# A wavelet-attention convolution block: the map convolution by six products for four outputs, with the next step's column filter in two lumps

## The chip, the cores and the metric

The kernel runs on one core of a Trainium2 chip. The metric is device time in microseconds (us) for one execution. Engines: PE (TensorE, matmuls; PEld is its weight load), DVE (VectorE), ACT (ScalarE), POOL (GpSimd), SP (SyncE, which only issues DMAs here).

## The reference, cut to what matters

```
# x: (8, 64, 224, 224); layer: x + block(group_norm(x)); W = H = 224, C = 64
res = conv3x3(x, W_id, b_id)                       # all 8 images
cA, cH, cV, cD = _swt2_level3(x[0])                # image 0 alone: row and column filters
high = jnp.stack([cH, cV, cD], axis=1).reshape(1, C3, H, W)
low_att = _attention(cA[None], DCT_LOW, ...)       # 1x1 convolution times a scale per channel
high_att = _attention(high, DCT_HIGH, ...)
dmt = jnp.concatenate([low_att, high_att], axis=1) # 256 channels
out = leaky_relu(conv3x3(dmt, W_enc, b_enc), 0.01) # one 64-channel map
return out + res                                   # the map is added to every image
```

The filtered image 0 has four subbands of 64 channels. The 3x3 convolution of these 256 channels to 64 gives the map `e_map` (128 lanes: 64 channels times 4 rows above, 4 rows below in a step), which the last stage adds to every image. "Map convolution" below is this one.

## The kernel before, in words

The program is three blocks one after the other, with a barrier between them.

`before_maps` (L204 to L710) filters image 0 along the rows on PE in four parts (`k`), writes the result to DRAM (`scratch`, the tensor `row_filtered`), and works out the attention scales and the merged convolution weights in small steps put between the filter's matmuls.

`encoder` (L713 to L930) makes the map in NE = 28 steps of ER = 8 rows. All engines walk through the steps in program order and meet by semaphores only. In step `step`:
- SP: `load(u)` (L752) brings the row-filtered rows of chunk `u = step + 2` into one of two buffers `s_in`; then `load_stats(k)` (L759) brings four pieces of the other seven images for their group-norm statistics, into two buffers `sx`. SP issues in this order and stands still at each wait: `load_stats(k)` waits until DVE has used piece `k - 2` (`stat_used`, L761), `load(u)` until POOL has split an earlier chunk (`s_split`, L777).
- POOL: `normalise` (L188; scale L199, bias L201) on chunk `u`, then the low half of its fp16 split (L928), after ACT's high half (`split_hi`, L844).
- PE: `gen` (L785, matmul L798), the column filter, makes one row of two subband pairs, 448 columns, in nine matmuls; eight rows a step, through a ring of four PSUM banks. Then `conv` (L802, matmuls L810 and L815) for q = 0, 1: 27 weight taps by two pairs, each on two column halves of the array, 448 columns each, and the bias.
- ACT `hi` (L839) and DVE `lo` (L874) turn each generated row into an fp16 pair in `d`; ACT carries the last two rows over (L861); ACT L869 and DVE L916 turn a finished accumulation into the leaky ReLU and store it in `e_map`.
- DVE `take_stats` (L879, statistics L885) works through four pieces a step, four instructions each.

`main` (L933 to L1173) runs the 3x3 convolution of all eight images and adds `e_map` to each. It is not touched.

What sets the order around the change is the queue of each engine as written, above all SP's:

```
for step in range(NE):
    u = step + 2
    ...
        load(u)
    for k in range(CPS * step, min(CPS * step + CPS, NCK)):
        load_stats(k)
```

Of the kernel before, what the change touches and what calls it, by code (L numbers as in the profile page):

```python
# [16 lines left out]
G = 32  # L17
# [23 lines left out]
EH = ER + 2  # L41
KEPT = HALF - 7 * (1 + 2 + 4)
# [21 lines left out]

def constants():
# [17 lines left out]
    fw = np.concatenate([low.T, high.T], axis=1)  # L83
# [16 lines left out]
    inside = np.zeros((TAPS, 3, W), np.float16)  # L100
    for t in range(TAPS):
        dy, dx = t // 3 - 1, t % 3 - 1
        inside[t, max(0, -dy):3 - max(0, dy), max(0, -dx):W - max(0, dx)] = 1.0
# [3 lines left out]
        "fw": np.stack([fw_hi, fw_lo], 1).reshape(2, HALF, 2, 2 * W).transpose(1, 0, 2, 3),  # L107
# [6 lines left out]
        "inside": inside.reshape(TAPS, 3 * W),  # L114
# [3 lines left out]
def conv_preact(nc, t, out):  # L118
# [4 lines left out]
    with ExitStack() as top:  # L123
# [6 lines left out]
        psum = [top.enter_context(nc.psum_tensor(f"ps{i}", [P, 512], F32)) for i in range(8)]  # L130
# [13 lines left out]
        rows_out = [sem(top, f"rows_out{k}") for k in range(2)]  # L144

        with ExitStack() as mid:
            shared = [sb(mid, f"shared{k}", [P, TAPS * C]) for k in range(2)]
            weff = [m[:, :].bitcast(F16).rearrange("p (s t e) -> p s t e", s=2, t=TAPS) for m in shared]
            bw = sb(mid, "bw", [P, C], F16)
            e_max = sb(mid, "e_max", [P, 2])  # L150
            b_part = sb(mid, "b_part", [P, 1])
# [9 lines left out]
            s_first = carve(HALF, 2 * ER * P, F32, "w (h r e) -> w h r e", h=2, r=ER)  # L161
            fw = carve(HALF, 2 * 2 * W, F16, "w (h b n) -> w h b n", h=2, b=2)
            halo = carve(HALF, 2 * P, F32, "w (h r e) -> w h r e", h=2, r=1)
            assert at[0] <= 2 * GS
            s_in = [s_first, carve(HALF, 2 * ER * P, F32, "w (h r e) -> w h r e", h=2, r=ER)]
            s_hl = carve(HALF, 2 * ER * P, F16, "w (h r k e) -> w h r k e", h=2, r=ER, k=2)
            halo_hl = carve(HALF, 2 * P, F16, "w (h k e) -> w h k e", h=2, k=2)
            free_at = at[0]
            assert 4 * GS <= free_at <= 5 * GS - 18 * C
            d_even = carve(P, 2 * EH * WP, F16, "p (b r s w) -> p b r s w", b=2, r=EH, s=2)  # L170
            scale_row = sb(mid, "scale_row", [P, C])
            bias_row = sb(mid, "bias_row", [P, 2, C])

            with ExitStack() as pre:
                u_sum = sb(pre, "u_sum", [HALF, 2, C, NG])
                mv = sb(pre, "mv", [HALF, C, 2])
                names = ["ident", "gw", "of_mean", "pick", "dsum", "wd_low", "wd_high", "bd", "w1_low", "w1_high",
                         "w2_low", "w2_high", "wa_low", "wa_high", "ba", "enc_low", "enc_high", "b_both"]
                c3 = {n: sb(pre, n, list(t[n].shape)) for n in names}
                before_maps(nc, x, t, scratch, psum, sb, sem, rows, rows_out, xg, pool_of, free_at, u_sum, mv, names, c3, partner, fw, halo, s_in,  # L180
                            s_hl, halo_hl, shared, w_hi, w_lo, w_max, b_id, scale_row, bias_row, norm_all, weff, bw, e_max, b_part)

            encoder(nc, x, t, scratch, rows_out, psum, sb, sem, weff, bw, e_max, b_part, early, e_map, mv_all,
                    fw, s_in, s_hl, halo_hl, d_even, scale_row, bias_row)
# [3 lines left out]
def normalise(engine, signal, count, v, scale_row, bias_row):  # L188

    if v.shape[2] == 1:  # L190
        vs, vb = [v.rearrange(p, s=2) for p in ("w h r (s c) -> w (h r s) c", "w h r (s c) -> w (h r) (s c)")]
    elif v.shape[2] == ER:
# [11 lines left out]
def before_maps(nc, x, t, scratch, psum, sb, sem, rows, rows_out, xg, pool_of, free_at, u_sum, mv, names, c3, partner, fw, halo, s_in,  # L204
                s_hl, halo_hl, shared, w_hi, w_lo, w_max, b_id, scale_row, bias_row, norm_all, weff, bw, e_max, b_part):


    with ExitStack() as s1:
        fh = sb(s1, "fh", [HALF, 2, NS1])
        records = sb(s1, "records", [HALF, C, 2, 6])  # L210
        w32, wn = [m[:, :].rearrange("p (t e) -> p t e", t=TAPS) for m in shared]
        wmx = sb(s1, "wmx", [P, 2])
        winv = sb(s1, "winv", [P, 1])
        ones = sb(s1, "ones", [HALF, P])
        mhalf = sb(s1, "mhalf", [P, 1])
        pair = sb(s1, "pair", [P, 2, G])
        gmean = sb(s1, "gmean", [P, G, 2])
        dev = sb(s1, "dev", [HALF, 2, C])
        gvar = sb(s1, "gvar", [P, G, 2])
# [11 lines left out]
        einv = sb(s1, "einv", [P, 1])  # L231
# [6 lines left out]
        b32, bn = [shared[1][:, C * k:C * k + C] for k in (4, 5)]  # L238

        spot = 3 * GS  # L240
        was_low = pool_of[0:C, spot:spot + C]
        was_high = pool_of[0:96, spot + C:spot + 7 * C].rearrange("p (g n) -> p g n", g=2)
        brow = pool_of[0:1, spot + 7 * C:spot + 16 * C]
        e32, en = [pool_of[:, free_at + 18 * C * k:free_at + 18 * C * (k + 1)].rearrange("p (s n) -> p s n", s=2) for k in range(2)]
# [7 lines left out]
        second_in = sem(s1, "second_in")  # L252
# [28 lines left out]
        e_done = sem(s1, "e_done")  # L281
        brow_ready = sem(s1, "brow_ready")
# [3 lines left out]
        einv_ready = sem(s1, "einv_ready")  # L286
        high_ready = sem(s1, "high_ready")
        first_high = sem(s1, "first_high")
        N0 = 2 * HR + NG
        HN = TAPS * C // 2  # L290
# [6 lines left out]
        def place(n):  # L297
# [5 lines left out]
        after = {"mean": 3, "variance": 9, "project": 15, "weigh": 23, "squeeze": 29, "excite": 33, "bias": 41,  # L303
                 "weights0": 47, "weights1": 51, "weights2": 55, "weights3": 59}
# [3 lines left out]
        with nc.Block() as block:  # L308
            @block.sync
            def _(sp):  # L310
# [6 lines left out]
                def write(k):  # L317
# [3 lines left out]
                    sp.dma_start(scratch[wc, :, HR * hh:HR * hh + HR, :].rearrange("w r e -> w (r e)"),  # L321
                                 rows[hh].rearrange("w r s c -> w (r s c)")).then_inc(rows_out[hh], 16)
# [21 lines left out]
                sp.dma_start(fw, t["fw"]).then_inc(fw_in, 16)  # L344
                sp.wait_ge(rows_out[0], 32)
                for wc in range(2):
                    sp.dma_start(halo[:, wc, :, :], scratch[wc, :, 0:1, :]).then_inc(first_in, 16)
                    sp.dma_start(s_in[0][:, wc, :, :].rearrange("w r e -> w (r e)"),
                                 scratch[wc, :, 1:ER + 1, :].rearrange("w r e -> w (r e)")).then_inc(first_in, 16)

                sp.wait_ge(brow_ready, 2)
                sp.dma_start(b32[0:TAPS, :], brow.rearrange("a (t e) -> a t e", t=TAPS)).then_inc(b32_in, 16)
                for wc in range(2):
                    sp.dma_start(s_in[1][:, wc, :, :].rearrange("w r e -> w (r e)"),
                                 scratch[wc, :, ER + 1:2 * ER + 1, :].rearrange("w r e -> w (r e)")).then_inc(second_in, 16)
                write(LAST)
                sp.wait_ge(fw_in, 16)
                sp.wait_ge(first_in, 64)
                sp.wait_ge(second_in, 32)

            @block.tensor
            def _(pe):
# [52 lines left out]
                def bias():  # L415
                    pe.wait_ge(was_ready, 6)
                    for n in range(2):
                        cols = slice(n * HN, n * HN + HN)
                        o = psum[6 + n][0:1, 0:HN]
                        pe.matmul(o, bs[0:C, 0:1], c3["enc_low"][:, cols], start=True, stop=False)  # L420
                        for g in range(2):
                            mm = pe.matmul(o, bs[:, 1 + g:2 + g], c3["enc_high"][:, g, cols], start=False, stop=(g == 1))
                    mm.then_inc(e_done, 1)

                def weights(k):
                    sw, n = k // 2, k % 2
                    cols = slice(n * HN, n * HN + HN)
                    if k == 2:
                        pe.wait_ge(brow_ready, 2)
                    for sh in range(2):  # L430
                        o = psum[4 + k][C * sh:C * sh + C, 0:HN]
# [44 lines left out]
            def _(act):  # L476
                def excite():
                    act.wait_ge(sc_done, 1)
                    act.activation(sg[0:C, 0:1], low_bank[0:C, 260:261], ACT.Sigmoid).then_inc(sig_done, 1)
                    act.activation(sg[:, 1:3], low_bank[0:96, 261:263], ACT.Sigmoid).then_inc(sig_done, 1)  # L480

                for k in range(4):
# [3 lines left out]
                    for c in range(0, C, 2):  # L486
# [9 lines left out]
                        if k == LAST and c + 1 == after["excite"]:  # L496
                            excite()
                act.wait_ge(product, 4 * C)
                act.wait_ge(e_done, 5)
                act.wait_ge(b32_in, 16)  # L500
                act.wait_ge(normal, 4)
                act.copy(halo_hl[:, :, 0, :], halo[:, :, 0, :]).then_inc(first_high, 1)
                act.copy(s_hl[:, :, :, 0, :].rearrange("w h r e -> w (h r) e"),
                         s_in[0][:, :, :, :].rearrange("w h r e -> w (h r) e")).then_inc(first_high, 1)
                act.wait_ge(einv_ready, 1)
                act.activation(weff[0][:, :, :, :].rearrange("p s t e -> p s (t e)"), e32, ACT.Identity,
                               scale=einv[:, 0:1]).then_inc(high_ready, 1)

            @block.vector
            def _(dve):  # L510
# [27 lines left out]
                gm = gmean[:, :, :].rearrange("p g a -> p (g a)")  # L538
# [12 lines left out]
                def variance():  # L551
# [3 lines left out]
                    dve.tensor_tensor_reduce(masked[:, 1, :], gvar[:, :, :].rearrange("p g a -> p (g a)"), c3["ident"][:, :],  # L555
# [44 lines left out]
                def excite():  # L600
                    dve.wait_ge(sig_done, 2)
                    dve.tensor_scalar(was_low, c3["wa_low"][:, :], sg[0:C, 0:1], None, ALU.mult).then_inc(was_ready, 1)
# [613 lines left out]
```

## Time and profile before

| | us |
|---|---|
| median of 3 runs | 2208.15 (2202.99 to 2209.74) |
| profiled execution | 2206.73 |
| its span | 2204.9 |
| `before_maps` | 0 to about 219.7 |
| `encoder` | 219.7 to about 1022 |
| `main` | about 1022 to 2204.9 |

The span is the stretch from the first to the last instruction of the profiled execution; 1.8 us of its time lie around it. The blocks' ends are read from the timeline: the first matmul of the next block.

### The profile page before, as it was taken

What the parts mean: (1) busy time and instruction counts of PE and PEld (TensorE: products, weight loads), DVE (VectorE), ACT (ScalarE), POOL (GpSimd) and SP (SyncE); (2) the same over time, 40 slices, a digit from 0 to 9 for tenths busy, and PEclk for the clock granted to TensorE, in tenths of its full rate; (3) what the DMA queues carried; (4) which work ended last, traced back from release to release, by engine and by line L of the source; (5) the groups of instructions that cost most, each with busy time, mean ns of one, the idle gap of its engine ahead of it and who ended that gap; (6) DMA issues with size and microseconds to landing.
All of it is one profiled execution on the core that took longest, in us unless ns stands there. A gap on an engine that the chain in (4) does not pass through costs nothing.

```text
span 2204.9 us, 74566 instructions
## 1 busy us (share of the span) xinstructions
PE 2132.9 (97%) x33526; PEld 1521.1 (69%) x33526; DVE 1435.6 (65%) x2235; ACT 823.5 (37%) x765; POOL 878.9 (40%) x543
## 2 busy tenths in 40 slices
PE   8997799999999999997999999999999999999998
PEld 7894566666666666664767776677677876677776
DVE  6755455555555555522777777777777777777776
ACT  3432333333333333322344344344444443444442
POOL 0001544444444444510444444444444444444444
PEclk9987899999999999998999999999999999999999
DMA  7942777777777777603687787887888878878874
GB/s 182 307 148 84 193 166 162 166 164 164 166 164 164 165 163 163 139 2 83 172 202 196 201 208 196 203 206 199 206 206 200 205 200 206 203 197 205 206 196 141
DMA packets 109191, 391.38 MB, mean 178 GB/s; under 512 B 45513, under 2 KB 46056, under 8 KB 95144
## 3 DMA queue, kind: packets, MB, share of 16 engines
q1 hardware_dynamic: 108904, 386.89, 70.3%
q8 instruction: 262, 4.29, 0.9%
q14 instruction: 25, 0.20, 0.0%
HBM read 258.37 MB, written 128.45 MB: 175 GB/s over the span
## 4 chain that ended last, share of the span: by engine, by line
issue 30%; POOL 23%; POOLq 1%; DVE 0%; PE 0%
POOL stage L1172 23%; POOLq L1170 1%; PE ps L1151 0%; POOLq L1165 0%; DVE dev L1107 0%; DVE gsum L1111 0%; DVE quad L1101 0%; DVE gsum L1104 0%; DVE dev L1110 0%; DVE dev L1109 0%; DVE quad L1103 0%; DVE gvar L1112 0%; DVE gmean L1105 0%; POOL root L1164 0%; POOLq L1163 0%
## 5 line engine op out<-in xcount | busy, mean ns | idle before, releaser
L1172 POOL TENSOR_TENSOR stage<-stage,big 128x448 f32<-128x448 f32 x448 | 511.1, 1141 | 661.5 <-DVE stage L1078 661.5
L1078 DVE SCALAR_TENSOR_TENSOR stage<-ps,w_max,xs 64x448 f32<-64x448 f32 x832 | 568.2, 683 | 79.3 <-PE ps L1146 55.0
L1146 PE MATMUL ps<-x_hi,w_hi 64*64 64x448 f16 x8064 | 454.0, 351 | 18.2 <-issue 18.0
L1036 ACT ACTIVATE x_hi<-xs,norm_now 128x2240 f16<-128x2240 f32 x104 | 234.9, 2258 | 608.5 <-PE ps L1146 605.8
L1146 PE MATMUL ps<-x_hi,w_lo 64*64 64x448 f16 x8064 | 451.0, 350 | 0.1
L1146 PEld LDWEIGHTS ps<-x_hi,w_hi 64*64 64x64 f16 x8064 | 294.8, 107 | 125.0 <-issue 23.5
L1146 PEld LDWEIGHTS ps<-x_hi,w_lo 64*64 64x64 f16 x8064 | 294.6, 107 | 106.0 <-issue 3.4
L810 PE MATMUL ps<-d_odd,shared 128*64 128x448 f16 x3024 | 293.5, 353 | 0.0
L810 PE MATMUL ps<-pool_of,shared 128*64 128x448 f16 x3024 | 293.5, 353 | 0.0
L916 DVE SCALAR_TENSOR_TENSOR big<-ps,e_max,lin 128x448 f32<-128x448 f32 x56 | 38.3, 683 | 331.0 <-ACT lin L869 331.0
L810 PEld LDWEIGHTS ps<-d_odd,shared 128*64 128x64 f16 x3024 | 172.4, 109 | 114.6
L810 PEld LDWEIGHTS ps<-pool_of,shared 128*64 128x64 f16 x3024 | 172.1, 109 | 114.8
L199 POOL TENSOR_TENSOR pool_of<-pool_of,scale_row 112x2048 f32<-112x2048 f32 (+2 forms) x29 | 127.0, 4381 | 288.0 <-DMA pool_of<-row_filtered 273.2
L1040 ACT ACTIVATE xn<-xs,norm_now 128x2240 f32<-128x2240 f32 x104 | 233.0, 2241 | 0.0
L1146 PE MATMUL ps<-big,w_hi 64*64 64x448 f16 x4032 | 224.7, 350 | 0.0
L1146 PE MATMUL ps<-x_lo,w_hi 64*64 64x448 f16 x4032 | 224.6, 350 | 0.0
L798 PE MATMUL ps<-pool_of 112*128 112x322 f16 (+2 forms) x2016 | 198.8, 261 | 21.7 <-POOL pool_of L928 12.8
L885 DVE BATCH_NORM_STATS2 records<-big 128x6 f32<-128x448 f32 x392 | 212.3, 610 | 8.1 <-DMA big<-in_x 8.0
L869 ACT ACTIVATE lin<-ps,b_part,e_max 128x448 f32<-128x448 f32 x56 | 40.5, 723 | 465.5 <-PE ps L815 465.5
L798 PEld LDWEIGHTS ps<-pool_of 112*128 112x128 f16 x2016 | 164.0, 99 | 60.5 <-issue 31.3
L1057 DVE TENSOR_TENSOR x_lo<-xn,x_hi 128x2240 f16<-128x2240 f32 x56 | 139.7, 2495 | 95.6 <-ACT xn L1040 95.6
L1057 DVE TENSOR_TENSOR big<-xn,x_hi 128x2240 f16<-128x2240 f32 x56 | 139.7, 2495 | 91.2 <-ACT xn L1040 91.2
(176 smaller groups left out, 1739.7 us busy)
## 6 DMA issues: line engine op xcount, KB each, us to landing
xs<-in_x SPq DMA_DIRECT2D x200, 560.0 KB, 7.1
out<-stage SPq DMA_DIRECT2D x448, 224.0 KB, 3.1
big<-in_x SPq DMA_DIRECT2D x196, 448.0 KB, 7.4
row_filtered<-big SPq DMA_DIRECT2D x4, 6272.0 KB, 21.4
pool_of<-row_filtered SPq DMA_DIRECT2D x54, 448.0 KB, 9.9
pool_of<-in_x SPq DMA_DIRECT2D x32, 392.0 KB, 6.7
big<-in_x SPq DMA_DIRECT2D x8, 560.0 KB, 7.3
xs<-in_x SPq DMA_DIRECT2D x8, 504.0 KB, 7.3
```

Source lines behind the costliest of these rows:

```text
L199: engine.tensor_tensor(vs, vs, scale.broadcast_to(tuple(vs.shape)), ALU.mult).then_inc(signal, 1)
L798: mm = pe.matmul(o, lhs[:, wc, a, :], v, start=(k == 0), stop=(k == 8))
L810: pe.matmul(o[C * s:C * s + C, 0:NT], w, d[n][:, b, r:r + 2, sw, kx:kx + W], start=(k == 0), stop=False)
L869: act.activation(lin[:, q, :], psum[4 + 2 * (step % 2) + q][:, 0:NT], ACT.Identity, scale=e_max[:, 1:2], bias=b_part[:, 0:1]).then_inc(lin ...
L885: ins = dve.bn_stats(records[:, j % 2, PER * c + i, :], sx[k % 2][:, i * NT:i * NT + NT])
L916: dve.scalar_tensor_tensor(e_map[:, (2 * step + q) * NT:(2 * step + q + 1) * NT], psum[4 + 2 * (step % 2) + q][:, 0:NT], e_max[:, 0:1], li ...
L1036: act.activation(x_hi[p][:, :, 1:1 + W], xs[slot][:, :].rearrange("p (r w) -> p r w", w=W), ACT.Identity, scale=scale, bias=bias).then_inc ...
L1040: act.activation(xn[:, :], xs[slot][:, :], ACT.Identity, scale=scale, bias=bias).then_inc(xn_ready, 1)
L1057: ins = dve.tensor_tensor(x_lo[p][:, :, 1:1 + W], xn[:, :].rearrange("p (r w) -> p r w", w=W), x_hi[p][:, :, 1:1 + W], ALU.subtract)
L1078: dve.scalar_tensor_tensor(stage[p][o, r, g, :], psum[4 * p + 2 * g + r][o, 0:NT], w_max[lanes, 0:1], xs[slot][lanes, c:c + NT], ALU.mult, ...
L1146: mm = pe.matmul(psum[4 * p + 2 * g + r][C * k:C * k + C, 0:NT], w[lanes, t, :], v[lanes, y:y + 2, kx:kx + W], start=(j == 0), stop=(j == ...
L1172: pool.tensor_tensor(stage[p][:, r, g, :], stage[p][:, r, g, :], e_map[:, e:e + NT], ALU.add)\
```

## The change

The map convolution no longer runs its nine taps on the map itself. In the width it uses a transform that gives four outputs of a 3-tap filter from six products: `input_transform` gives the six combinations, and they are folded into the column filter's matrix `fw`, so that `gen` makes 6 x 56 = 336 columns for each subband pair (672 a row, before 448). The weights `u32` are the 3x3 weights at six points. `conv` makes, for each of the six products, three row taps by three fp16 pieces by two subband pairs, on two column halves, 224 columns each (4 rows by 56 tiles). The four outputs are put together after that from the products by DVE (`pairs`, `outer`), ACT (`scale`, `positive`, `put`) and POOL (`inner`, `leaky`).

A row of `gen` fills two PSUM banks, and the ring is two rows. Rows are loaded, normalised and split in chunks of CH = 4 rows, two a step. PE runs `gen` for four rows, products 1 and 2, `gen` for the other four, products 3 and 4, then 0 and 5. The statistics on DVE begin one step later: step `step` works through the four pieces `4 (step - 1)` to `4 (step - 1) + 3`. In `before_maps` the first rows are written to DRAM separately, so that the first chunks are loaded and split earlier; four multiplications of the attention scale move from DVE to ACT; the weights are made by more DVE instructions in 16 places.

The core of the diff (SP, PE, and the order on ACT, DVE and POOL):

```diff
+            def load(u):
+                if u == HALF // CH - 1:
+                    sp.wait_ge(rows_out[1], 32)
+                sp.wait_ge(s_split, u - 3)
+                for wc in range(2):
+                    sp.dma_start(s_in[u % 2][:, wc, 0:rows_of(u), :]...).then_inc(step_in[u % 2], 16)
...
                 for step in range(NE):
-                    u = step + 2
-                    if u < NE:
...
-                        load(u)
-                    for k in range(CPS * step, min(CPS * step + CPS, NCK)):
+                    for u in (2 * step + 4, 2 * step + 5):
+                        if u < NU:
+                            load(u)
+                    for k in range(CPS * step + 2, min(CPS * step + 2 + CPS, NCK)):
                         load_stats(k)
```

`load_stats` is as before: for `k >= 2` it waits for `stat_used >= k - 1`.

```diff
             def gen(tile, lhs):
-                    if tile >= 4:
-                        pe.wait_ge(lo_done, tile - 3)
...
+                    if tile >= 2:
+                        pe.wait_ge(lo_done, tile - 1)
+                    for sw in range(2):
...
+                        for k, (a, b) in enumerate(((0, 0), (0, 1), (1, 0))):
+                            pe.matmul(tiles(o)[:, :, 15:NTILE], lhs[:, 1, a, :], tiles(v)[:, :, 15:NTILE], ...)
+                        for k, (a, b) in enumerate(((0, 0), (0, 1), (1, 0))):
+                            pe.matmul(tiles(o)[:, :, 0:15], lhs[:, 0, a, :], tiles(v)[:, :, 0:15], ...)
+                            mm = pe.matmul(both(o), lhs[:, 0, a, :], both(v), ...)
...
+                    gens(range(min(CH, fresh(step))))
+                    pe.wait_ge(lo_done, FIRST + ER * step - (step == NE - 1))
...
+                    conv(step, 5, (1, 2))
+                    gens(range(CH, fresh(step)))
+                    conv(step, 6, (3, 4)).then_inc(conv_done, 1)
...
+                    conv(step, 4, (0, 5)).then_inc(conv_done, 1)
```

`gens` takes chunk `u = 2 * step + 2 + k // CH` and waits for its low half (`s_split >= u - 1`) at the first row of each lump.

```diff
             def _(act):
...
+                        act.wait_ge(conv_done, 2 * step)
+                        scale(step - 1)
                     for k in range(fresh(step)):
                         hi(tile_of(step, k), m, 2 + k)
+                        if step and k == 5:
+                            positive(step - 1)
...
+                    if 2 * step + 4 < NU:
+                        split_hi(2 * step + 4)
+                    if step:
+                        put(step - 1)
+                    if 2 * step + 5 < NU:
+                        split_hi(2 * step + 5)
+                    copy_second(step)
...
             def _(dve):
...
+                    now = 16 * (step - 1)
                     for k in range(fresh(step)):
                         lo(tile_of(step, k), m, 2 + k)
+                        if step and k % 2 == 1:
+                            stat(now)
+                            now += 1
+                        if step and k == 4:
+                            outer(step - 1)
...
+                    while step and now < 16 * step:
+                        stat(now)
+                        now += 1
+                    pairs(step)
...
             def _(pool):
...
                 for step in range(NE):
+                    if step:
+                        inner(step - 1)
+                    for u in (2 * step + 4, 2 * step + 5):
+                        if u < NU:
+                            normal_rows(u)
+                        if step and u % 2 == 0:
+                            leaky(step - 1)
+                    for u in (2 * step + 4, 2 * step + 5):
+                        if u < NU:
+                            split_lo(u)
```

One `stat` is one statistics instruction; four make a piece, and the fourth raises `stat_used`. `normal_rows(u)` is two POOL instructions on 112 x 1024 f32, `split_lo` one, `inner` four on 128 x 224, `leaky` one on 128 x 896. `pairs` is two DVE instructions on 128 x 448, `outer` two on 128 x 224; `scale` is three ACT instructions on 128 x 224, `positive` one on 128 x 896, `put` four on 128 x 224 written at a stride of four, `copy_second` one on 128 x 448. `hi` and `lo` now work on 128 x 672, the carry copy on 128 x 2688.

## Rows read from the trace of the kernel before

**Rows 1.** The page, sections 1 and 2: busy us, and tenths in 40 slices.
```profile
PE 2132.9 (97%) x33526; PEld 1521.1 (69%) x33526; DVE 1435.6 (65%) x2235; ACT 823.5 (37%) x765; POOL 878.9 (40%) x543
PE   8997799999999999997999999999999999999998
```
**Rows 2.** Windows: one step; the start of `main`. Busy us (instructions), clock, DMA, GB/s.
```profile
500.00:528.00 28.00, 28.00 (x296) 18.35 (x294) 14.93 (x27) 9.12 (x12) 13.21 (x4) 1.00 0.72 165
1037.79:1045.55 7.76, 7.76 (x108) 4.67 (x112) 2.50 (x1) 2.21 (x2) 0.00 (x0) 0.65 0.89 188
```
**Rows 3.** Timeline of PE in one step: start us, us, instructions.
```profile
272.92 6.93 PE L798 MATMUL ps<-pool_of 112*128 112x322 f16 x72
279.79 10.48 PE L810 MATMUL ps<-d_odd,shared 128*64 128x448 f16 x108
290.10 0.36 PE L815 MATMUL ps<-inside,bw 128*64 128x448 f16 x2
290.29 10.48 PE L810 MATMUL ps<-d_odd,shared 128*64 128x448 f16 x108
```
**Rows 4.** Waits, 270 to 960 us: total us, times, longest.
```profile
POOL pool_of L199 <- DMA pool_of<-row_filtered: 245.9, 24, 11.4
```
**Rows 5.** SP's own waits, 220 to 1020 us.
```profile
SPq L764 <- DVE records L885: 539.7, 96, 22.9
```
**Rows 6.** Groups by shape: count | busy us, mean ns of one | idle before.
```profile
L885 DVE BATCH_NORM_STATS2 records<-big 128x6 f32<-128x448 f32 x392 | 212.3, 610 | 8.1 <-DMA big<-in_x 8.0
L876 DVE TENSOR_TENSOR pool_of<-ps,pool_of 128x448 f16<-128x448 f32 x113 | 70.8, 627 | 24.1 <-ACT pool_of L841 22.9
L680 DVE TENSOR_TENSOR pool_of<-pool_of 112x2048 f16<-112x2048 f32 x1 | 2.3, 2282 | 0.0
L841 ACT CAST pool_of<-ps 128x448 f16<-128x448 f32 x113 | 60.4, 535 | 39.1 <-PE ps L798 34.6 <-DVE pool_of L897 4.5
L846 ACT CAST pool_of<-pool_of 112x2048 f16<-112x2048 f32 x27 | 51.3, 1901 | 6.0 <-POOL pool_of L201 6.0
L199 POOL TENSOR_TENSOR pool_of<-pool_of,scale_row 112x256 f32<-112x256 f32 x1 | 0.7, 725 | 27.3 <-DMA pool_of<-row_filtered 27.3
L199 POOL TENSOR_TENSOR pool_of<-pool_of,scale_row 112x2048 f32<-112x2048 f32 x27 | 122.3, 4531 | 260.7 <-DMA pool_of<-row_filtered 245.9 <-issue 14.8
L928 POOL TENSOR_TENSOR pool_of<-pool_of 112x2048 f16<-112x2048 f32 x27 | 110.4, 4087 | 130.7 <-ACT pool_of L846 130.7
```
**Rows 7.** Timeline of DVE: the statistics of step 0, two pieces, then one and one.
```profile
253.08 4.30 DVE L885 BATCH_NORM_STATS2 records<-big 128x6 f32<-128x448 f32 x8
263.92 2.19 DVE L885 BATCH_NORM_STATS2 records<-big 128x6 f32<-128x448 f32 x4
```
**Rows 8.** Issues and landing: L764 from 283 us, L764 from 285, L755 from 286.
```profile
L764 SPq DMA_DIRECT2D big<-in_x x2: 466/532/598, 283.2 to 283.7; - x2
DMA to landing us min/median/max: 4.4/5.1/5.9
...
L764 SPq DMA_DIRECT2D big<-in_x x2: 466/532/597, 285.3 to 285.8; - x2
DMA to landing us min/median/max: 6.3/7.1/7.9
...
L755 SPq DMA_DIRECT2D pool_of<-row_filtered x2: 427/504/581, 286.5 to 287.1; - x2
DMA to landing us min/median/max: 8.9/9.4/9.9
```
**Rows 9.** Timeline of PE at the start of `main`, after idle time.
```profile
1037.79 3.58 PE L1146 MATMUL ps<-x_hi,w_hi 64*64 64x448 f16 x36 [14.72 <-issue]
1041.12 2.91 PE L1146 MATMUL ps<-x_hi,w_lo 64*64 64x448 f16 x36
1043.84 1.89 PE L1146 MATMUL ps<-x_lo,w_hi 64*64 64x448 f16 x36
1045.55 1.89 PE L1146 MATMUL ps<-x_hi,w_hi 64*64 64x448 f16 x36
```
**Rows 10.** Timeline: PE at the encoder's start; DVE in `before_maps` beside POOL.
```profile
219.74 9.80 PE L798 MATMUL ps<-pool_of 112*128 112x322 f16 x81 [8.84 <-PEq L308]
242.38 9.55 PE L798 MATMUL ps<-pool_of 112*128 112x322 f16 x72 [12.85 <-POOL pool_of L928]
...
170.51 4.40 DVE L602 TENSOR_SCALAR pool_of<-wa_low,sg 64x64 f32<-64x64 f32 x1 [0.99 <-ACT sg L480]
174.84 4.84 DVE L604 TENSOR_SCALAR pool_of<-wa_high,sg 96x192 f32<-96x192 f32 x2
```

More of the change, by code:

```diff
@@ L62, with input_transform @@
 SUBBAND = [1, 2, 3]
+def input_transform():
+    at = np.array([[p ** k for p in NODES] + [1.0 if k == 3 else 0.0] for k in range(4)])
+    g = np.array([[p ** k for k in range(3)] for p in NODES] + [[0.0, 0.0, 1.0]])
+    system = np.array([at[m] * g[:, k] for m in range(4) for k in range(3)])
+    wanted = np.array([[float(j == m + k) for j in range(NI)] for m in range(4) for k in range(3)])
+    b = np.linalg.lstsq(system, wanted, rcond=None)[0]
+    b[np.abs(b) < 1e-12] = 0.0
+    b[5] /= STEP ** 3
+    return b
 def constants():
@@ L668, in _ @@
                             measure(g, cc)
-                        if k == LAST and c in stage_at:
+                        if k == LAST and stage_at.get(c) in stages:
                             stages[stage_at[c]]()
+                        for j in range(4):
+                            for part_no in range(4):
+                                if k == LAST and c == after[f"weights{j}"] + 2 * part_no - (2 if part_no == 3 and j == 3 else 0):
+                                    weights(j, part_no)
                     if k == 2:
@@ L849, in _, with put @@
-                act.wait_ge(pads_set, 7)
+                    act.wait_ge(s_ready, u - 1)
+                    act.wait_ge(gen_done, CH * (u - 1) + 1)
+                    act.copy(s_hl[u % 2][:, :, :, 0, :].rearrange("w h r e -> w (h r) e"),
+                             s_in[u % 2].rearrange("w h r e -> w (h r) e")).then_inc(s_high, 1)
+                def put(step):
+                    act.wait_ge(leaky_done, step + 1)
+                    o = e_map[:, step * EN:(step + 1) * EN].rearrange("p (n k) -> p k n", k=4)
+                    for k in range(4):
+                        ins = act.activation(o[:, k, :], z_of(step)[:, k, :], ACT.Identity, scale=e_max[:, k:k + 1], bias=b_id[:, 0:1])
+                    ins.then_inc(map_done, 1)
@@ L850, in _, with positive, copy_second @@
+                def positive(step):
+                    act.wait_ge(z_done, step + 1)
+                    act.activation(side_of(step), z_of(step), ACT.Relu, scale=99.0).then_inc(pos_done, 1)
+                def copy_second(step):
+                    act.wait_ge(conv_done, 2 * step + 1)
+                    if step:
+                        act.wait_ge(z_part, step)
+                    act.copy(ab[:, 1, :, :], ps[:, 5:7, MN:2 * MN]).then_inc(second_copied, 1)
                 for k in range(FIRST):
@@ L933, in main @@
+                inner(NE - 1)
+                leaky(NE - 1)
 def main(nc, x, out, psum, sb, sem, early, e_map, partner, mv_all, norm_all, w_hi, w_lo, w_max):
```

630 lines of the change are left out of this document (393 added, 237 removed).

## The prediction

> **What bounds the kernel now.** I read the page first. PE is busy 97% of the span, and its row of tenths is at 9 nearly everywhere [rows 1]. Then the windows: a step of the encoder takes 28.0 us and PE is busy in all of it, DVE in 14.9, ACT in 9.1, POOL in 13.2 [rows 2]. The timeline of PE shows what the step is made of: 6.87 us of column filter (72 matmuls, 272.92 to 279.79), then twice 10.5 us of convolution [rows 3]. So the encoder is bound by PE alone, and nothing that another engine does is late. The waits matter for the change: POOL stood 24 times for the row-filtered rows to land, 245.9 us in all, and PE never noticed, since a chunk is loaded more than a step before its rows are filtered [rows 4]. SP stood 539.7 us, 96 times, at the statistics' loads until DVE had used a piece [rows 5]. So the queue that brings the rows is held by DVE's statistics most of the time, and only the distance of over a step covers that.
>
> **PE's own work after the change.** Column filter: 72 matmuls with 8 x 1932 columns take 6.87 us, 0.444 ns a column [rows 3]. A new row has 2 x 3 x (246 + 90 + 168) = 3024 columns in 18 matmuls, so 1.32 us (1.26 to 1.5), and eight rows 10.6 us: plus 3.7. Convolution: 110 matmuls of 448 columns take 10.5 us, that is 191 ns for a pair on the two column halves [rows 3]. With 224 columns a pair streams in half; I take 98 ns (95 if the fixed part halves too, 191 if the weight loads set the pace). A product is 18 pairs, 19 with bias: 1.76 to 1.86 us; six are 11.0 us against 21.0. PE has 21.6 us a step instead of 28.0. By this alone 28 steps would give back some 180 us.
>
> **The other engines' pieces.** From pairs of sizes [rows 6]: ACT's `hi` on 672 elements 0.72 us (535 ns at 448, 1901 at 2048, so 0.83 to 0.85 ns an element); DVE's `lo` 0.86 (627 ns at 448, 2282 at 2048, 1.03 an element); POOL's two-input instruction 0.18 us plus 2.12 ns an element (725 and 4531 ns at 256 and 2048), so 2.36 us on 1024 and 4.7 for a normalisation, 2.1 for `split_lo` (half of 4087 ns and a little), 2.1 for `leaky`, 0.66 for each of `inner`. Sums in a step: POOL 18.4, ACT about 16, DVE about 18. None is above PE. But the ring of two rows now ties them: the third row of a lump waits until the first is read out, 1.32 + 0.2 + 0.72 + 0.04 + 0.86 + 0.1 = 3.24 us after its start (the small terms are hand-overs I estimate), where two rows take PE 2.64. A lump of four is 5.9 us instead of 5.3.
>
> **The order on SP, which decides.** Count the pieces. SP's step s loads the chunks 2s+4 and 2s+5, then the pieces 4s+2 to 4s+5; the last of these waits until piece 4s+3 is used. DVE now uses the pieces 4s to 4s+3 in its step s+1, the last three of them after the last `lo` of that step. So SP issues the load of chunk 2s+6 only when DVE's statistics of step s+1 are over. PE needs this chunk, normalised and split, for the first row of step s+2. The distance of over a step is gone: filter rows of a step, then statistics, then load, normalise, split, then filter rows of the next step. Nothing in this ring overlaps, so the step's time is its sum:
>
> - first lump 5.9 us, plus 0.6 because the first `hi` stands behind `scale`, plus 2.0 for the clock. In `main`, after 14.7 us of idle PE, the first two groups of 36 matmuls take 3.33 and 2.72 us from start to start, where later ones take 1.71, with a granted clock of 0.65: 2.6 us lost on the way from 1.2 to 2.4 GHz [rows 2, 9]. In the ring PE would stand some 30 us each step, so it pays this each step; a part hides in the ring of two. 8.5 (5.3 to 10.6);
> - products 1 and 2: 3.7 (3.5 to 5);
> - second lump, with `outer` between two of its `lo`: 6.2 (5.5 to 7);
> - last `hi`, `lo` and the fourth statistic: 0.2 + 0.72 + 0.04 + 0.86 + 0.54 = 2.4;
> - twelve statistics at 0.54 us (4.30 us for eight [rows 7]) are 6.5 us, if the data is there. One piece is, two are not: the first of them is issued at the last `lo` and the second when the first three pieces' buffer comes free, 2.2 us later. In the rows a piece on a free queue (two DMAs, issued at 283.2 and 283.7) is there 5.9 us after the second, 6.4 after the first; the piece behind it (285.3 and 285.8) 7.9 after its second, 8.4 after its first [rows 8]. So they run from 6.4 to 8.6 and from 10.6 to 12.8: 12.8 (8.6 to 15);
> - the rows' landing: 2688 KB (two pieces and a chunk of 2 x 448) landed by 297.0 (287.1 + 9.9), 13.8 us after the first issue at 283.2 [rows 8], 228 KB a us beyond 2 us that I take as fixed. Here two pieces, of which one was issued 4.2 us earlier, and 2 x 224 KB: 2240 / 228 + 2 - 4.2 = 7.6, with SP's issue 8.0 (5.4 to 11);
> - POOL: normalise 4.7, `leaky` 2.1, normalise the other chunk 4.7, `split_lo` 2.1: 13.6 (13 to 15). `split_hi` and `put` on ACT hide behind these.
>
> Sum 55.2 us, against 28.0. The loads held are those of the chunks 6, 8, ... 52, that is 24 steps: 24 x (55.2 - 28.0) = +653 us. The last pieces (98 in all) are loaded in SP's step 23, so the steps after 25 run free.
>
> The DMA part of this rests on the in-order queue [rows 5]. The Trainium skill, "DMA: Bandwidth & Descriptors", "Anatomy of one DMA — SWDGE (gpsimd) path", says that DMA engines don't wait on semaphores and that a wait is taken by the issuing sequencer before dispatch. By this rule the load behind a waiting `load_stats` can't start early. The trace agrees: the row-filtered issues come only behind the second piece's (286.5 after 285.8) [rows 8].
>
> On the clock, the trace shows the slow start after idle time [rows 9]. The Trainium skill, "TensorE: Matmul & The Clock Gate", "Part 1: The HAM clock gate", calls the throttled state the default, which activity releases. By it every round starts at 1.2 GHz, the 2.0 us above; if the clock stayed up the sum would be 53.2 us and the time 48 us less.
>
> **What else changes.** In `before_maps` two DVE multiplications took 9.2 us beside POOL and PE stood behind them [rows 10]; they go to ACT: up to -9. The weights take some 32 DVE instructions of 0.4 to 0.5 us instead of 8: +8, less what hides; the tail is shorter by about 5. At the encoder's start PE waited 12.85 us for POOL and its first step began 22.6 us after the first row [rows 10]; with nine rows at 1.6 us and chunks split earlier about 14: -8. Four steps outside the ring (0, 1, 26, 27) gain 2 to 4 us each: -10. After the last product a chain of `pairs`, `scale`, `inner`, `outer`, `positive`, `leaky`, `put` adds 5 to 8 us. Together -20 (-40 to +15). Everything goes against the profiled 2206.7: 2206.7 + 653 - 20 = 2840; the median lies 1.4 us higher: 2841. `main` stays.
>
> **Rivals.**
> 1. The change does what PE's sums say, and the ring is not closed: the rows land in time. Then ACT's chain sets the step: after the last `hi` carry 2.4, `split_hi` 1.05, `put` 2.5, `split_hi` 1.05, then `copy_second` 0.5, `pairs` 1.3, `scale` 1.4, the first `hi` and `lo` 1.6, gives about 25.4 us: 24 x -2.6 - 20 = -82, about 2125. For it: PE's rows, and that POOL's waits cost nothing before [rows 4]. Against it: the count of pieces. It decides at a ring of 28.8 us; even without any wait for DMA in the statistics, with a landing of 5.4 and a full clock, the ring is 44. So it needs the ring not to exist. Chance 0.05.
> 2. The ring's short end: one statistics wait of two hides, landing 5.4, no clock loss: 5.9 + 3.5 + 5.5 + 2.2 + 8.6 + 5.4 + 13 = 44.1, +386 - 30: about 2563. The cases up to 50 us a round belong here. Chance 0.14.
> 3. The long end: PE slow for the whole first lump and the products, DMAs slower with 2 KB pieces a partition: 10.6 + 5 + 7 + 2.4 + 15 + 11 + 15 = 66, +912: about 3110. Cases over 60 us belong here. Chance 0.11.
>
> **Forecast and chances.** The likeliest case, rounds of 50 to 60 us, has 0.70 and its own range 2700 to 2950. The range that should hold 8 in 10 reaches into both ends: 2600 to 3020. What a measurement can tell from no change is about 0.3%, 7 us. Slower 0.95 (forecast and rivals 2 and 3), faster 0.04, within 0.3% 0.01 (rival 1, and what I have overlooked).
>
> **What would show it.** In the profile after: encoder steps of 50 to 60 us from step 2 to 25 and of 23 to 27 outside; PE idle some 30 us a step in front of the first row, put down to POOL's `split_lo`; POOL's first normalisation waiting for the row-filtered DMA, whose issue stands right behind the last statistics; two DMA waits a step in the statistics; PE's clock below 1 in the encoder. A product of 1.8 us and a row of 1.3 us would prove PE's part. Steps near 25 us with PE busy in 85% would refute the ring.

## The result, and the profile after

The changed kernel takes 2839.16 us (median of four runs, 2834.41 to 2840.1) against 2207.59 for the kernel before, a ratio of 1.286 [1.2835, 1.2885]. The forecast was 2841, from a ring in which filter rows, statistics, landing, POOL's work and the next filter rows follow one another. The profiled execution took 2834.41 us with a span of 2832.6. A "round" below is one step of the encoder while the ring is closed, and the "landing" is the time from the end of the round's last statistic to the start of POOL's first normalisation.

The page after, sections 1 and 2, stands against [rows 1]. PE has fallen from 97% to 72% of the span, and the 18 slices from a tenth of the span to 55% of it, all in the encoder, stand at 3 to 5.

```profile
PE 2030.1 (72%) x35664; PEld 1633.4 (58%) x35664; DVE 1495.2 (53%) x2310; ACT 988.9 (35%) x1003; POOL 1020.1 (36%) x769
...
PE   8997345335434533553354669999999999999998
...
PEclk9988667667766776776677889999999999999999
```

One round of the encoder by windows (busy us and instruction counts of PE, PEld, DVE, ACT, POOL, then clock, DMA share, GB/s) answers to the step of 28.00 in [rows 2]. PE is busy for 24.7 us of 54.6; the window leaves out the last 1.2 us of the round, which is 55.75 us long.

```profile
802.90:857.50 54.60, 24.66 (x368) 22.56 (x368) 18.21 (x28) 14.46 (x20) 16.84 (x11) 0.72 0.36 85
```

The waits between 320 and 1600 us (total us, times, longest) name the ring's links, and SP's own come last:

```profile
POOL pool_of L250 <- DMA pool_of<-row_filtered: 859.0, 24, 38.8
...
PE ps L937 <- POOL pool_of L1159: 693.9, 23, 31.1
...
DVE pool_of L1091 <- DMA big<-in_x: 147.7, 46, 5.2
```

```profile
SPq L907 <- DVE pool_of L1091: 1120.8, 92, 40.2
```

The first of these existed before and cost nothing [rows 4]: 24 times, up to 11.4 us. It now lasts up to 38.8 us, and PE stands behind it 23 times, 30 us each (L1159 is POOL's `split_lo`, L937 the first filter matmul). Two DMA waits a round in the statistics (46 in 23 rounds) are the two that the prediction counted.

The timeline of one round, engine by engine (start, us, instructions, and in brackets the idle time before and what ended it), is the ring itself. Start with DVE, at the last `lo` (L1079). L1096 is the sum over one image's statistics, which comes once in fourteen pieces and here stands in the time of the first DMA wait:

```profile
821.78 0.86 DVE L1079 TENSOR_TENSOR pool_of<-ps,pool_of 128x672 f16<-128x672 f32 x1 [0.53 <-ACT pool_of L1001]
822.56 2.72 DVE L1091 BATCH_NORM_STATS2 pool_of<-big 128x6 f32<-128x448 f32 x5
825.31 1.67 DVE L1096 BATCH_NORM_AGGREGATE mv_all<-pool_of 128x2 f32<-128x336 f32 x1
829.83 2.20 DVE L1091 BATCH_NORM_STATS2 pool_of<-big 128x6 f32<-128x448 f32 x4 [2.85 <-DMA big<-in_x]
834.56 2.20 DVE L1091 BATCH_NORM_STATS2 pool_of<-big 128x6 f32<-128x448 f32 x4 [2.52 <-DMA big<-in_x]
```

SP issues the piece loads (L907) between 823.20 and 837.89, each when a buffer comes free, the last pair at the end of the statistics (836.76). The load of the rows (L898) stands right behind:

```profile
823.20 14.69 SPq L907 DMA_DIRECT2D big<-in_x  x8
837.94 1.99 SPq L898 DMA_DIRECT2D pool_of<-row_filtered  x4
```

POOL then waits for the landing, and works through normalise, `leaky` (L1178), normalise, `split_lo`:

```profile
844.96 2.34 POOL L250 TENSOR_TENSOR pool_of<-pool_of 112x1024 f32<-112x1024 f32 x1 [37.60 <-DMA pool_of<-row_filtered]
847.38 2.34 POOL L252 TENSOR_TENSOR pool_of<-pool_of 112x1024 f32<-112x1024 f32 x1
849.68 2.07 POOL L1178 TENSOR_TENSOR big<-big 128x896 f32<-128x896 f32 x1
851.71 2.36 POOL L250 TENSOR_TENSOR pool_of<-pool_of 112x1024 f32<-112x1024 f32 x1
854.14 2.34 POOL L252 TENSOR_TENSOR pool_of<-pool_of 112x1024 f32<-112x1024 f32 x1
856.44 4.21 POOL L1159 TENSOR_TENSOR pool_of<-pool_of 112x1024 f16<-112x1024 f32 x2
```

And PE: a row of `gen` is two groups of nine matmuls, of which the first three of a group stand here. First the round's first row, its groups 1.29 us apart at half clock; then a product and its bias (L950) at full clock; then the second lump's first two rows, and its third.

```profile
802.87 0.81 PE L937 MATMUL ps<-pool_of 112*128 112x246 f16 x3 [30.49 <-POOL pool_of L1159]
...
804.16 0.83 PE L937 MATMUL ps<-pool_of 112*128 112x246 f16 x3
...
812.88 1.89 PE L962 MATMUL ps<-d_odd,shared 128*64 128x224 f16 x36
814.61 0.26 PE L950 MATMUL ps<-pool_of 128*64 128x224 f16 x2
...
814.80 0.50 PE L937 MATMUL ps<-pool_of 112*128 112x246 f16 x3
815.50 0.49 PE L937 MATMUL ps<-pool_of 112*128 112x246 f16 x3
...
816.19 0.49 PE L937 MATMUL ps<-pool_of 112*128 112x246 f16 x3
...
818.06 0.50 PE L937 MATMUL ps<-pool_of 112*128 112x246 f16 x3 [0.32 <-DVE pool_of L1079]
```

Warm, a group takes 0.69 us and a row 1.39; at half clock 1.3 and 2.6. The third row starts 3.26 us after the first. The next round's first row stands at 858.62, 55.75 us after this one's.

### The profile page after: what moved, and what is told of

Its sections match the earlier page's. It is cut to its first block and busy times, and to the rows that moved or that the text cites. A ratio compares the mean times of both kernels' runs of the same rounds, so it can differ in the third digit from the quotient of the medians.

```text
span 2832.6 us, 79514 instructions
## 1 busy us (share of the span) xinstructions
PE 2030.1 (72%) x35664; PEld 1633.4 (58%) x35664; DVE 1495.2 (53%) x2310; ACT 988.9 (35%) x1003; POOL 1020.1 (36%) x769
## 5 line engine op out<-in xcount | busy, mean ns | idle before, releaser
L937 PE MATMUL ps<-pool_of 112*128 112x246 f16 x1344 | 252.4, 302 | 751.7 <-POOL pool_of L1159 724.8
L937 PEld LDWEIGHTS ps<-pool_of 112*128 112x128 f16 x1344 | 128.5, 108 | 784.4 <-POOL pool_of L1159 730.5
L250 POOL TENSOR_TENSOR pool_of<-pool_of 112x1024 f32<-112x1024 f32 (+2 forms) x57 | 131.8, 2312 | 935.7 <-DMA pool_of<-row_filtered 923.7
L1091 DVE BATCH_NORM_STATS2 pool_of<-big 128x6 f32<-128x448 f32 x392 | 220.1, 613 | 154.3 <-DMA big<-in_x 154.3
L1101 DVE TENSOR_TENSOR pool_of<-ps,pool_of 128x448 f32<-128x448 f32 x28 | 17.5, 624 | 526.3 <-ACT pool_of L1038 526.3
L1006 ACT CAST pool_of<-pool_of 112x1024 f16<-112x1024 f32 x54 | 56.4, 1047 | 669.2 <-POOL pool_of L252 669.2
L941 PE MATMUL ps<-pool_of 112*128 112x168 f16 x1344 | 244.6, 263 | 0.0
L940 PE MATMUL ps<-pool_of 112*128 112x90 f16 x1344 | 226.5, 221 | 0.0
L1412 PEld LDWEIGHTS ps<-big,w_hi 64*64 64x64 f16 x4032 | 146.9, 107 | 52.2
L1412 PEld LDWEIGHTS ps<-x_lo,w_hi 64*64 64x64 f16 x4032 | 146.5, 107 | 52.3
```

The source lines that it names most:

```text
L250: engine.tensor_tensor(vs, vs, scale.broadcast_to(tuple(vs.shape)), ALU.mult).then_inc(signal, 1)
L937: pe.matmul(tiles(o)[:, :, 15:NTILE], lhs[:, 1, a, :], tiles(v)[:, :, 15:NTILE], start=(k == 0), stop=False)
L940: pe.matmul(tiles(o)[:, :, 0:15], lhs[:, 0, a, :], tiles(v)[:, :, 0:15], start=False, stop=False)
L941: mm = pe.matmul(both(o), lhs[:, 0, a, :], both(v), start=False, stop=(k == 2))
L1006: act.copy(s_hl[u % 2][:, :, :, 0, :].rearrange("w h r e -> w (h r) e"), s_in[u % 2].rearrange("w h r e -> w (h r) e")).then_inc(s_high, 1)
L1091: ins = dve.bn_stats(records[:, PER * (k % NCH) + i, :], sx[k % 2][:, i * NT:i * NT + NT])
```

## The experiments

Each was run in turns with the kernel before on its chip, and the ratio is to that. "Step" is the mean interval between the starts of ACT's `copy_second` over steps 1 to 24. It is 28.0 us before and 55.5 after.

### The order on SP: four pieces earlier, and two

```diff
-for k in range(CPS * step + 2, min(CPS * step + 2 + CPS, NCK)):
+for k in range(max(2, CPS * step - 2), min(CPS * step - 2 + CPS, NCK)):
     load_stats(k)
```

The runs go by short names: e1 is this one, four pieces. For e2, two pieces, the range is from `max(2, CPS * step)` to `min(CPS * step + CPS, NCK)`.

> The changed kernel, but SP issues each step's two row loads four statistics pieces earlier in its queue (the piece in front of them is one that DVE uses a step earlier). Theory (the ring over SP's queue: last statistics, row load, POOL, column filter): the ring of 55.5 us is cut, PE no longer waits some 30 us for POOL's split. Next in line is DVE: its last statistics end 12.8 us after the last lo, then pairs 1.2, scale 1.0, first hi and lo; a step of about 32 us, total 2839 - 24 x 23.3 = about 2280. Rival A (two row buffers and POOL's 13.6 us of work in sequence are the ring, whatever SP's order): steps of about 42 us, total about 2520. Rival B (the row loads are late because the DMA queues are full, not because of the order of issue): total above 2750.

> The same with the row loads two pieces earlier only. Theory: the loads go out when the second of the four pieces is used, 2.2 us after the last lo, instead of after the fourth at 12.8; the ring loses these 10.6 us and gets 1.3 back, because two pieces are issued around the load: about 46 us a step, total about 2610. Rival A: no difference to the run with the loads four pieces earlier. Rival B: total above 2750.

Measured: four pieces earlier 2331.92 us, ratio 1.0536 [1.0509, 1.0563], step 34.4; two pieces 2643.73 us, 1.1954 [1.1924, 1.1985], step 47.5. Only the place of the same loads in one queue differs, nothing of the arithmetic, and 507 of the 632 us are gone with the larger shift. That the rows' load queued behind the statistics is the cause is thereby shown. With two pieces the time is 34 us over my 2610, and the step 1.5 us over my 46. The Trainium skill, "DMA: Bandwidth & Descriptors", "Anatomy of one DMA — SWDGE (gpsimd) path", says that the issuing sequencer takes a DMA's wait before dispatch. The section is about DMAs that GpSimd issues and these are issued by SP, but both runs agree with it: the earlier the loads stand in SP's order, the shorter the step, 47.5 and 34.4 us for 55.5.

The kernel with four pieces earlier is still slower than the one before. I had expected that, but it is 52 us above my 2280. A window of one step, then DVE's timeline, ACT's and PE's, show what is late next:

```profile
591.20:625.20 34.00, 24.18 (x367) 22.21 (x364) 18.10 (x30) 14.35 (x20) 17.86 (x11) 0.85 0.60 139
```

```profile
614.56 2.21 DVE L1091 BATCH_NORM_STATS2 pool_of<-big 128x6 f32<-128x448 f32 x4 [3.01 <-DMA big<-in_x]
619.30 2.21 DVE L1091 BATCH_NORM_STATS2 pool_of<-big 128x6 f32<-128x448 f32 x4 [2.54 <-DMA big<-in_x]
621.42 0.61 DVE L1101 TENSOR_TENSOR pool_of<-ps,pool_of 128x448 f32<-128x448 f32 x1
...
624.30 1.62 DVE L1079 TENSOR_TENSOR d_odd<-ps,d_odd 128x672 f16<-128x672 f32 x2 [1.74 <-ACT d_odd L1001]
```

```profile
622.64 0.95 ACT L1026 ACTIVATE big<-pool_of 128x224 f32<-128x224 f32 x3 [9.42 <-issue]
623.50 1.32 ACT L1001 CAST d_odd<-ps 128x672 f16<-128x672 f32 x2
```

```profile
625.21 0.81 PE L937 MATMUL ps<-pool_of 112*128 112x246 f16 x3 [9.04 <-DVE d_odd L1079]
```

The statistics and their two DMA waits still end the step on DVE. `pairs` (L1101) stands behind them, ACT's `scale` (L1026) behind `pairs`, the first `hi` behind `scale`, and PE's third row waits 9.04 us for the first `lo`. After that gap the clock is down again (0.81 us for the three matmuls that take 0.49 warm), which my 32 us a step had left out.

### The statistics without their transfers

```diff
             sp.wait_ge(stat_used, k - 1)
+            return
...
-            dve.wait_ge(stat_in[k % 2], 32 * (k // 2) + 32)
+            dve.wait_ge(stat_in[k % 2], 32)
```

It leaves out the transfers of all pieces but the first two, so DVE works on those again and again, and what it gets for images 1 to 7 is not their statistics. SP's waits stay.

> The changed kernel, without the transfers of the statistics' pieces beyond the first two: SP still waits for every piece to be used, DVE works on the same two buffers again and again (the statistics of images 1 to 7 are not those of the reference). It measures what the DMA waits in the statistics and the queue in front of the rows cost: theory: twelve statistics take 6.5 us instead of 12.8, the rows land in about 4.5 instead of 8.2, SP needs 1 us less; the ring 45 us, total about 2590. Rival (order alone, the DMAs cost nothing): unchanged at 2839.

Measured: 2574.39 us, 1.1641 [1.1611, 1.1671], step 44.4. The DMA waits inside the statistics and the landing behind two pieces are 11.1 of the 27.5 us that a round has too much. The other 16 stay, with SP's order and no other traffic: the ring is not a shortage of bandwidth. I had expected 45 us a step and 2590.

### One lump

```diff
-        gens(range(min(CH, fresh(step))))
+        gens(range(fresh(step)))
...
-        gens(range(CH, fresh(step)))
```

> The changed kernel with the column filter of the next step in one lump of eight rows ahead of all six products. Theory: in the ring of 55.5 us products 1 and 2 (3.8 us) fall out of the path, and the row ring costs 2.6 us of PE wait more in the longer lump less what the break gave: 52 to 53 us a step, total 2750 to 2780. Rival B (the split into two lumps is what costs, since the two chunks are normalised one after the other and the first lump waits for both): the loss goes away for most part, total under 2500.

Measured: 2769.4 us, 1.2523 [1.2489, 1.2556], step 52.6. The two lumps that the change is about cost 2.9 us a round while the ring is closed, since products 1 and 2 (3.8 us) stand between the first lump and the `lo` after which the statistics end. They are a tenth of the loss.

### PE kept busy in the gap

```diff
         conv(step, 4, (0, 5)).then_inc(conv_done, 1)
+        if 1 <= step <= 24:
+            for _ in range(150):
+                pe.matmul(psum[7][0:64, 0:448], fw[:, 0, 0, 0:64], fw[:, 0, 0, 0:448], start=True, stop=True)
```

> The changed kernel, with 150 extra matmuls of 448 columns (64 lanes out, into a free PSUM bank) after the last product of steps 1 to 24, some 28 us of PE work in the 30 us in which PE stands. It measures the clock term of the ring alone: theory: the clock stays at 2.4 GHz, the first four rows take 5.9 to 6.2 us instead of 8.2, the ring is 53.5 us and the total 2839 - 24 x 2.0 = 2791. Rival (the first lump is slow because its first hi stands behind scale, not by the clock): unchanged within 10 us, or longer where the extra matmuls end after POOL's split.

Measured: 2841.27 us, 1.2863 [1.2826, 1.2901], step 55.7: no gain, and a miss of 50 us. The added matmuls filled 28.5 us of each gap, and 1.3 to 4.0 us were left. That was enough for the clock to be down at some point of the first lump in 16 of 23 rounds. The timeline shows a round that starts cold after a gap of 2.68 us, and one that starts warm after 2.58; the windows show the granted clock of both first lumps:

```profile
754.32 0.81 PE L937 MATMUL ps<-pool_of 112*128 112x246 f16 x3 [2.68 <-POOL pool_of L1162]
```

```profile
922.33 0.50 PE L937 MATMUL ps<-pool_of 112*128 112x246 f16 x3 [2.58 <-POOL pool_of L1162]
```

```profile
754.30:761.80 7.50, 7.49 (x57) 0.58 0.00 0
...
922.20:928.40 6.20, 5.68 (x72) 1.00 0.01 1
```

0.58 over the first window is mostly 1.2 GHz, 1.00 is 2.4. In the seven warm rounds the first lump took 6.19 us and the round 54.0; in the others 8.1 and 56.4. So the clock is worth what the prediction gave it, but the experiment did not remove its cause. The rival that I gave, that `scale` and not the clock makes the first lump slow, foretold this total and is still wrong: `scale` stands in front of the warm lumps too. The landing was also longer, 9.05 us instead of 8.39. By the issues between 320 and 1600 us, a piece landed in 6.2 us (median; 6.0 in the changed kernel), a chunk's half in 7.0 (6.6). That the added matmuls are the reason is not shown: in e4, which has none and the same order on SP, the landing is 8.82 us, a piece lands in 6.2 us and a chunk's half in 6.9.

### The ring taken apart, and the statistics spread

The order on SP is that of e1, and on DVE:

```diff
-        if step and k % 2 == 1:
+        for _ in range((3 if k == 3 else 1) if step else 0):
             stat(now)
             now += 1
```

> The run with the row loads four pieces earlier, and DVE's sixteen statistics of a step spread: one after each row's lo, two more after the fourth (in the time of products 1 and 2), six after the last instead of twelve. Theory: the step of 34.2 us was set by the 12.8 us from the last lo to the end of the statistics, in which two pieces had to be fetched; with six left only one fetch lies there and most of it hides. Then ACT's own row of work after the last hi (carry, two splits, put) and the row ring set the step at 25 to 27 us, PE stands 4 to 5 us and loses little clock; total 2839 - 24 x 29.3 = about 2140, 3% below the kernel before. Rival (PE's clock, not DVE, holds the step: it falls in every gap and costs 3 us or more): above 2200.

> The same with the column filter in one lump of eight rows. Theory: with the ring over SP gone, the statistics have no product gap to run in, but PE's products all come last and cover ACT's and DVE's chain after the last row; I expect a step up to 1 us shorter than with two lumps, total 2105 to 2140. Rival (the split in two lumps is worth having, because the row ring of two starves PE in a long lump): 1.5 us a step longer, total 2170 to 2190.

Measured: 2112.49 us, 0.9562 [0.9535, 0.9589], step 25.2; with one lump of eight rows besides 2094.66 us, 0.9478 [0.9451, 0.9506], step 24.5. The transform and the six products are in these kernels unchanged. What made the changed kernel 29% slower was the place of two loops: one in SP's queue, one in DVE's. Spreading the statistics with SP's order left as it was has not been run. Both times are below what I expected, 2140 and 2105 to 2140.

In e5 the step's end looks like this on ACT (carry, `split_hi`, `put`, `split_hi`, `copy_second`), on DVE (the last statistics, `pairs`), and on PE, whose third row waits for the first `lo`:

```profile
626.02 2.44 ACT L1061 COPY pool_of<-d_odd 128x2688 f16<-128x2688 f16 x1
628.36 1.05 ACT L1006 CAST pool_of<-pool_of 112x1024 f16<-112x1024 f32 x1
629.30 2.46 ACT L1013 ACTIVATE big<-big,b_id,e_max 128x224 f32<-128x224 f32 x4
631.54 1.08 ACT L1006 CAST pool_of<-pool_of 112x1024 f16<-112x1024 f32 x1
632.51 0.53 ACT L1038 COPY pool_of<-ps 128x448 f32<-128x448 f32 x1
```

```profile
630.79 2.21 DVE L1091 BATCH_NORM_STATS2 pool_of<-big 128x6 f32<-128x448 f32 x4 [2.18 <-DMA big<-in_x]
633.08 0.62 DVE L1101 TENSOR_TENSOR pool_of<-ps,pool_of 128x448 f32<-128x448 f32 x1
```

```profile
636.88 0.50 PE L937 MATMUL ps<-pool_of 112*128 112x246 f16 x3 [0.90 <-DVE d_odd L1079]
```

In all 23 steps ACT has no idle time from the last `hi` to the end of `copy_second` (7.62 us), and the statistics end within 0.5 us of it, before or after. So two chains reach `pairs` together; in three of the steps the sum L1096 then holds `pairs` for another 1.6 to 2.0 us.

### Six rows and two, one product between

Both edits of e5, and in the order on PE:

```diff
-        gens(range(min(CH, fresh(step))))
+        gens(range(min(6, fresh(step))))
...
-        conv(step, 5, (1, 2))
-        gens(range(CH, fresh(step)))
+        conv(step, 5, (1,))
+        gens(range(6, fresh(step)))
+        conv(step, 5, (2,), 1)
```

The new last argument of `conv` is only the PSUM place of the product.

> The run with the row loads four pieces earlier and the statistics spread, with the column filter in lumps of six and two rows and product 1 between them. Theory: with nothing late from outside, the step of 24.5 us in the one-lump run is PE's own: 13.7 us for eight rows, of which 3.1 are waits in the ring of two, and 10.9 of products. Product 1 (1.8 us) covers one wait of some 0.8 us and ACT's tail begins no later; a step of 23.6 to 24.2 us, total 2068 to 2088. Rival (the row waits come with every pair of rows wherever the products stand, so nothing is won): 2095 within 0.3%.

Measured: 2067.15 us, 0.9364 [0.934, 0.9387], step 23.4, just under the range that I expected: the fastest, ahead of both kernels. Page and one step by windows:

```profile
PE 1973.5 (96%) x35664; PEld 1600.4 (78%) x35664; DVE 1487.5 (72%) x2310; ACT 978.6 (48%) x1003; POOL 1025.7 (50%) x769
```

```profile
602.58:626.00 23.42, 22.61 (x369) 21.18 (x370) 16.93 (x29) 14.61 (x21) 17.81 (x11) 1.00 0.86 202
```

PE is busy for 22.61 of 23.42 us at full clock, and the two gaps left are 0.4 us each, in the ring of two rows. So PE bounds the step again, as it did before the change.

### One lump, rows first, statistics not spread

Both edits are shown above: the order on SP of e1, and the one lump of e4.

> The run with the row loads four pieces earlier, the column filter in one lump, the statistics as in the changed kernel (twelve after the last lo). It completes the square of lumps and spread. Theory: the step goes from the last lo over 15 us of statistics with two fetches to pairs, scale and the next first row; in one lump products 1 and 2 lie behind the rows, beside the statistics, and fall out of this chain too: 34.4 less 3.8 to 5: 29.5 to 30.5 us, total about 2215 to 2240. Rival (the lumps matter only while SP's ring is closed): 34.4 us a step and 2332 as with two lumps.

Measured: 2251.94 us, 1.0197 [1.0163, 1.0232], step 31.0, 12 us over the upper end of what I expected. With one lump, spreading the statistics is worth 6.5 us a step (31.0 to 24.5), with two lumps 9.2 (34.4 to 25.2). SP's order alone, without it, makes no version faster than before.

## Why the prediction was right, step by step

The ring's terms are means over 23 rounds, each read from the timelines as in the round above. The landing has SP's issue in it:

| term, us | predicted | after | e3, no transfers |
|---|---|---|---|
| first lump | 8.5 | 8.12 | 8.29 |
| products 1, 2 | 3.7 | 3.77 | 3.76 |
| second lump | 6.2 | 6.13 | 6.13 |
| last `hi`, `lo` and all statistics | 2.4 + 12.8 = 15.2 | 1.72 + 13.69 = 15.41 | 1.72 + 7.09 = 8.81 |
| landing | 8.0 | 8.39 | 3.72 |
| POOL | 13.6 | 13.66 | 13.67 |
| sum | 55.2 | 55.47 | 44.38 |

- **The order on SP decides.** Right, and shown by e1 and e2. Read from PE's busy sums alone, the change would have been some 180 us faster.
- **The statistics' two waits.** The twelve statistics behind the fourth were predicted at 12.8 us, 6.3 of it waits, from one landing of 6.4 and one of 10.6; with the last `hi` and `lo` the row came within 0.2 us. The two DMA waits are 147.7 us in 23 rounds, 6.4 a round. Without transfers (e3) the thirteen instructions take 6.85 us, or 8.69 in the three rounds in which L1096 stands among them. The prediction left L1096 out; with the transfers it lies in the time of a DMA wait.
- **The landing.** The rate of 228 KB a us from [rows 8], with 2 us taken as fixed, gave 8.0 against 8.39. With 448 KB alone they give 4.0, and 4.4 with SP's issue, against 3.72 in e3. No run shows the 2 us by themselves.
- **The clock.** Predicted 2.0 us a round in the first lump. Warm first lumps in e7 take 6.19, those of the changed kernel 8.12, so 1.9. The 0.6 us for `scale` in front of the first `hi` was too much: in the warm first lumps of e7 the third row starts 3.33 us after the first, in the second lumps, which have no `scale`, 3.26, so it costs 0.07. A warm lump without it takes 6.13 instead of 5.9, by the longer rows.
- **PE's own pieces.** A row takes 1.39 us warm (1.32 forecast; 3024 columns at the 0.444 ns of [rows 3] are 1.34), its third in a lump starts after 3.26 (3.24), and a product with bias takes 1.85 (1.76 to 1.86), from 811.03 to 812.88. The 18 pairs from 812.88 to 814.61 take 96 ns each, against 191 with 448 columns: the time halves with the columns, so the weight loads don't set the pace at 224.
- **What else changes** was forecast at -20 us and came to -32. By the first filter matmul of the encoder (200.43 after, 219.74 before) `before_maps` gave 19.3 instead of about 6:

```profile
197.02 0.35 PE L548 MATMUL ps<-fh,pool_of 112*112 112x98 f32 x2
200.43 0.79 PE L937 MATMUL ps<-pool_of 112*128 112x246 f16 x3 [3.07 <-PEq L369]
```

Its row filter ends at 197.4 instead of 210.9. Some 7 us of these 13.5 are idle time of PE: the wait of 7.7 us behind the DVE multiplications of [rows 10] is gone (there are three, not two as the prediction says, and five move to ACT in all). The other 6.5 us are the clock, a term that the prediction did not have. In that wait the granted clock fell to its lower level, 1.2 GHz, and stayed there for 17 us; in the changed kernel it stays up to the end of the row filter. Before, then after:

```profile
176.20:193.30 17.10, 12.98 (x35) 6.78 (x36) 7.28 (x13) 1.06 (x2) 3.36 (x1) 0.50 0.00 0
```

```profile
158.60:197.40 38.80, 38.21 (x244) 29.79 (x242) 21.89 (x75) 18.31 (x42) 15.69 (x9) 1.00 0.22 67
```

The added DVE work for the weights, 0.2 to 0.6 us each, hid between the filter's copies; I had let most of it count. The tail behind it is 3.1 us for 8.8. The encoder outside the ring gave 12.1 us by the blocks' ends, forecast at about 12 (-8, -10 and +6); the three parts were not measured one by one. The ring was 24 x 0.27 = 6.5 us more than its 653: 2204.9 + 659.3 - 19.3 - 12.1 - 0.2 (`main`) = 2832.6, the span.
- **Luck.** The mechanism was right, and each term of the ring came within 0.4 us. That 2839 came within 2 us of 2841 was luck: the ring was 6.5 us longer than forecast and the rest gained 12 us more, and the median lies 4.8 us above the profiled execution where 1.4 was taken.
- **Rival 1** (a step of 25.4 if the ring didn't exist) is what e5 measures once the ring is taken out: 25.2 us, and 2112 against 2125. The chain that rival 1 names is there: in the step shown, 10.7 us from the end of the last `hi` (626.13) to the end of the first `lo` (636.83), for 11.8 listed. But the statistics on DVE end together with ACT's part of it, and which of the two would hold the step alone is not shown; e8 gets under it by PE's order alone. **Rivals 2 and 3** fell with the terms above: both statistics waits show in every round, and the landing came 0.4 us above its estimate, not 3.

## What to carry to other kernels

Where one queue carries transfers for two consumers, and one of its entries waits for a consumer's progress, count in entries how far each load is ahead of its use, after the change as well as before. If the consumer moves later by one step, every load behind it moves too. Four entries' shift of one loop was worth 507 us here, while the new arithmetic in the best order tried is 141 us ahead of the kernel before. A consumer that is not urgent (the statistics) is best spread through the step: in one block at its end it holds whatever comes first in the next one.

## What the runs showed of the hardware that I had not expected

- With PE busy until 1.3 to 4.0 us before a round, the granted clock was down during 16 of 23 first lumps; after 2.68 us of idle time one round started at half clock and after 2.58 another stayed at full clock, so the length of the last gap alone does not tell the outcome.
- A single wait of 7.7 us on PE in `before_maps` was followed by 17.1 us at a granted clock of 0.50, and cost some 6.5 us beside itself: with the wait gone, the row filter ran at 1.00 and PE's busy time to its end was 183.5 us instead of 190.0.
